# Two adaLN transformer layers, main attention: the place of the next heads' query weights (their fetch and their split) moved by one prepared block

## The chip, the cores and the metric

The kernel runs on one core of one Trainium2 chip. The metric is the time of one execution on the device in microseconds; the median of three runs is given. All times inside the program are counted from the start of the profiled span.

## The reference

One call computes two transformer layers on an input of 1024 rows by 256. Only the first half of the first layer matters here, its main attention over 16 heads:

```python
q = (q_mid @ q_b_w.T).reshape(b, s, H, D_Q).transpose(0, 2, 1, 3)
q_nope, q_pe = (q[..., :D_NOPE], q[..., D_NOPE:])
kv_lora, k_pe_flat = (kv_a[..., :KVR], kv_a[..., KVR:])
...
q_pe = apply_rope(q_pe, cos, sin)
k_pe = apply_rope(k_pe, cos, sin)
qf = jnp.concatenate([q_nope, q_pe], -1)
kf = jnp.concatenate([k_nope, k_pe], -1)
scores = jnp.einsum('bhqd,bhkd->bhqk', qf, kf) * scale
probs = jax.nn.softmax(scores.astype(jnp.float32), axis=-1).astype(dt)
ctx = jnp.einsum('bhqk,bhkd->bhqd', probs, v)
main_out = ctx.transpose(0, 2, 1, 3).reshape(b, s, H * D_V) @ o_w.T
```

Here s is 1024, H 16, D_NOPE 128, D_ROPE 64. A pattern attention before it, a gated feed-forward of eight experts behind it and the whole second layer are not touched.

## The kernel before

**Tiles and units.** The main attention goes by pairs of heads, p = 0 to 7, and within a pair by four units of 256 queries each, so units u = 0 to 31 with p = u // 4. A unit has four score tiles (two heads, two times 128 queries) of 128 by 1024. For a tile PE multiplies queries with keys in three passes (L1834 to L1836: high with high, high with low, low with high), DVE takes the maxima (`nmq`, L1843), ACT exponentiates (`P`, L1858), DVE turns the result (`PT`, L1871), and PE multiplies it with the values (L1938). ACT and DVE join the two parts (L1949, L1957), DVE weighs them (L1963), PE projects (L1972), DVE adds to `x` (L1985).

**Prepared blocks.** The scores work on latent queries and keys of 128 rows per head: 64 from the latent part and 64 rotary ones. They are prepared for one pair while the pair before is in hand, in six blocks of 128 by 512, in this order: R0, R1 (rotary keys, two halves of the columns), R2 (rotary queries, first half), Q0 (latent queries, first half), R3, Q1 (second halves). In the code this is `FIRST`, k = 0 to 5. For each block

- PE computes the product (`pe_prep`, L1569) once the split weights are there: `wkh`/`wkl` for R0 and R1, `wqh`/`wql` for R2 and R3, `lth`/`ltl` for Q0 and Q1;
- ACT copies it from its bank to a staging tile `t` (L1623), of which there are two, taken in turn;
- for a rotary block SP issues four DMAs that swap rows of 32 within the tile (L1637), behind the copy;
- POOL (`pool_product`) multiplies by the cosine (L1650), by the sine behind the swap (L1652), adds (L1655), and writes the high halves (L1669) and low halves (L1676) of two heads, `qk1h`/`qk1l` for keys and `qk0h`/`qk0l` for queries. Latent blocks have the last two steps only.

The score tiles of pair p begin with score(4p, 0). It waits (`pe_score`) for R0, R1, R2 and Q0 of the pair, high and low; the second half of the queries, score(4p + 2, 0), waits for R3 and Q1.

**The order.** `main_order` writes out one list, MAIN, and each engine walks it and takes what is its own. With `PREP_AT = (5, 8, 9, 12, 16, 17)` the product of block k of pair p stands at score tile 16(p − 1) + PREP_AT[k]: R0 in unit 4p − 3, R1 and R2 in unit 4p − 2, Q0 in unit 4p − 1, R3 and Q1 in unit 4p. In a unit the order is

```python
order.append(("score", u, 0))
output(u - 2)
prep(4 * u, "prep")
order.extend([("rec", u - 1), ("spread", u - 1), ("vturn", u - 1, 3), ("expo", u, 0)])
prep(4 * u, "pcopy")
```

and then the tiles 1 to 3 with the two halves of the value product of unit u − 1. "rec" is DVE's row of reciprocals (`rrow`) and SP's four DMAs that gather it (`shares`, L1906); "spread" is SP's two DMAs that spread it to `Rs` (L1919), behind the first. SP's queue is strictly in order: the swap of a block stands behind the shares and the spread of its unit. POOL does not follow MAIN for this part. It has its own loop over pairs and blocks (`gpsimd`), so it is only as far as its own work and waits let it.

**The weights.** `wks` and `wqs` hold 128 by 256 of rotary weights of one pair, fetched by one DMA each (`sp_weights_k`, `sp_weights_q`) behind PE's last use of the ones before. POOL splits them into `wkh`, `wkl` (L1736, L1738) and `wqh`, `wql` (L1745, L1747); the latent weights are split into `lth`, `ltl` (L1756, L1758). The semaphore `wt_ok` counts the splits in the order key, latent, query of each pair.

Of the kernel before, what the change touches and what calls it, by code (L numbers as in the profile page):

```python
# [307 lines left out]
def program(nc, a, out):  # L308
# [1217 lines left out]
    def pool_mc(e, l):  # L1526
        e.wait_ge(ht_mm, 8 + 8 * l)
        e.memset(mc[0][:].bitcast(F32), 0.0).then_inc(mc_ok, 1)
        e.memset(mc[1][:].bitcast(F32), 0.0).then_inc(mc_ok, 1)
        e.wait_ge(mc_ok, 2 * l + 2)  # L1530
        if l:
            e.memset(mc[0][:, :, 96:99].bitcast(F32), 1.0).then_inc(mc_ok, 1)
            e.memset(mc[1][:, :, 96:99].bitcast(F32), 1.0).then_inc(mc_ok, 1)
# [186 lines left out]
    def sp_weights_k(e, p):  # L1720

        if p:
            e.wait_ge(rp_mm, 4 * p - 2)
        e.dma_start(wks[:], a["wkpe"][p]).then_inc(d_wk, 16)

    def sp_weights_q(e, p):

        if p:
            e.wait_ge(rp_mm, 4 * p)
        e.dma_start(wqs[:], a["wqpe"][p]).then_inc(d_wq, 16)  # L1730
# [10 lines left out]
    def pool_weights_q(e, p):  # L1741
        e.wait_ge(d_wq, 16 * (p + 1))
        if p:
            e.wait_ge(rp_mm, 4 * p)
        e.tensor_copy(wqh[:], wqs[:]).then_inc(wt_hi, 1)  # L1745
        e.wait_ge(wt_hi, SPLIT2["q", p])
        e.tensor_tensor(wql[:], wqs[:], wqh[:].bitcast(F32), ALU.subtract).then_inc(wt_ok, 1)  # L1747
        e.wait_ge(wt_ok, SPLIT2["q", p])

    def pool_weights_l(e, p):  # L1750
        if p:
            e.wait_ge(lt_mm, 2 * p)
        else:
            e.wait_ge(fold_ok, 6)
            e.wait_ge(d_below, 32)
        e.tensor_copy(lth[:], wab[:, :, 2 * p:2 * p + 2, :].rearrange("p a h c -> p a (h c)")).then_inc(wt_hi, 1)  # L1756
        e.wait_ge(wt_hi, SPLIT2["lat", p])
        e.tensor_tensor(ltl[:, :, p, :], wab[:, :, 2 * p:2 * p + 2, :].rearrange("p a h c -> p a (h c)"), lth[:].bitcast(F32), ALU.subtract).then_inc(wt_ok, 1)  # L1758
        e.wait_ge(wt_ok, SPLIT2["lat", p])
# [116 lines left out]
    def sp_values(e):  # L1876

        e.wait_ge(sh_mm, 16)
        e.wait_ge(pv_mm[0], 128)
        for s in range(4):  # L1880
            for g in range(4):
                e.dma_start(kv4[s][32 * g:32 * g + 32, :, :], kvx[32 * s:32 * s + 32, :, :]).then_inc(d_kv, 16)
# [1146 lines left out]
    def gpsimd(e):  # L3029
        pool_mc(e, 0)  # L3030
        pool_stack2(e, slice(0, 4))
        pool_vx_ones(e, 0)
        pool_latents(e)
        e.wait_ge(qkv_ok, NT)
        e.wait_ge(fold_ok, 6)
        pool_stack2(e, slice(4, 8))
        pool_rounded(e)
        pool_weights_k(e, 0)
        pool_weights_q(e, 0)
        pool_weights_l(e, 0)  # L3040
        e.wait_ge(neg_ok, 8)
        pool_scale(e)
        for p in range(8):
            if p < 2:
                pool_keys(e, p)
            for k in range(len(FIRST)):
                pool_product(e, p, k)
                if k == 0 and p:
                    pool_weights_q(e, p)
                elif k == 3 and p < 7:  # L3050
                    pool_weights_k(e, p + 1)
                elif k == 5 and p < 7:
                    pool_weights_l(e, p + 1)
        for s in MAIN:
            if s[0] == "wup":
                pool_scale_down(e, s[1])
            elif s[0] == "wdown":
                pool_split_down(e, s[1])
            elif s == ("hT", 0):
                pool_hT1(e)  # L3060
            elif s[0] == "hidden":
                pool_up0(e, *s[1:])
        e.wait_ge(dn_mm, downs_done(5))
        pool_vx_ones(e, 1)
        pool_mc(e, 1)
        for s in CAUSAL:
            if s[0] == "omm":
                pool_op_gate(e, s[1])
            elif s[0] == "split":
                pool_split1(e, s[1])  # L3070
            elif s[0] == "turn3":
                pool_hTh3(e)
        pool_fill1(e)
        for s in FINAL:
            if s[0] == "omm":
                pool_op_gate(e, s[1])
            elif s[0] == "split":
                pool_split1(e, s[1])
            elif s[0] == "hid" and KIND[s[1]] is None:
                pool_hidden1(e, *s[1:])  # L3080

    def sync(e):
        e.dma_start(idf[:], a["idf"]).then_inc(d_c, 16)
        e.dma_start(cc[:], a["cc"]).then_inc(d_c, 16)
        for i in range(2):
            e.dma_start(x[:, 4 * i:4 * i + 4, :], x_v[:, 4 * i:4 * i + 4, :]).then_inc(d_x[i], 16)
        e.dma_start(wm0[:, :, 0:512], a["wmod0"][:, :, 0:512]).then_inc(d_moda, 16)
        e.dma_start(wsp[:, 0:2, :, :], a["wsp0"][:, 0:2, :, :]).then_inc(d_w, 16)
        e.dma_start(owT[:], a["owT"]).then_inc(d_w3[0], 16)
        e.dma_start(kvbv[:], a["kvbv"]).then_inc(d_w3[0], 16)  # L3090
        e.dma_start(wm0[:, :, 512:1536], a["wmod0"][:, :, 512:1536]).then_inc(d_modb, 16)
        e.dma_start(w0a[:], a["w0a"]).then_inc(d_w2, 16)
        e.dma_start(lnw[:, 0:192], a["q_ln"].partition_broadcast(128)).then_inc(d_w2, 16)
        e.dma_start(lnw[:, 192:256], a["kv_ln"].partition_broadcast(128)).then_inc(d_w2, 16)
        e.dma_start(gsb[:], a["gate_b"].partition_broadcast(128)).then_inc(d_w2, 16)
        e.dma_start(wsp[:, 2:4, :, :], a["wsp0"][:, 2:4, :, :]).then_inc(d_wv, 16)
        sp_scratch2(e, 0)
        sp_scratch2(e, 1)
        sp_stack2(e, 0)
        e.dma_start(qbn[:], a["qbn"]).then_inc(d_w3[1], 16)  # L3100
        e.dma_start(kvbk[:], a["kvbk"]).then_inc(d_w3[1], 16)
        for d, n in ((idb, "idb"), (maskq, "maskq"), (maskk, "maskk"), (tri, "tri")):
            e.dma_start(d[:], a[n]).then_inc(d_k, 16)
        sp_stack2(e, 1)
        e.wait_ge(gate_mm, 4)
        e.wait_ge(gate_v, 8)
        sp_weights_k(e, 0)
        sp_weights_q(e, 0)
        sp_scratch2(e, 2)
        sp_scratch2(e, 3)  # L3110
        sp_stack2(e, 2)
        e.dma_start(cosT[:], a["cosT"]).then_inc(d_cs, 16)
        e.dma_start(sinT[:], a["sinT"]).then_inc(d_cs, 16)
        sp_below(e)
        for k in range(len(FIRST)):
            sp_swap(e, 0, k)
            if k == 2:
                sp_weights_k(e, 1)
        sp_values(e)
        for s in MAIN:  # L3120
            if s[0] == "pcopy":
                sp_swap(e, s[1], s[2])
                if s[2] == 0:
                    sp_weights_q(e, s[1])
                elif s[2] == 2 and s[1] < 7:
                    sp_weights_k(e, s[1] + 1)
            elif s[0] == "rec":
                if s[1] == 28:
                    e.wait_ge(st_mm[1], 16 * 7)
                    e.dma_start(wr[:], a["wr"]).then_inc(d_f, 16)  # L3130
                    e.dma_start(tmpr[:, 0:1], a["temp"].partition_broadcast(128)).then_inc(d_f, 16)
                    for x_ in range(2):
                        sp_expert0(e, x_)
                sp_shares(e, s[1])
            elif s[0] == "spread":
                sp_spread(e, s[1])
        for x_ in range(2, 4):
            sp_expert0(e, x_)
        e.wait_ge(*MAIN_DONE)
        e.dma_start(wm1[:], a["wmod1"]).then_inc(d_moda, 16)  # L3140
        e.wait_ge(ht_mm, 16)
        e.dma_start(w1a[:], a["w1a"]).then_inc(d_w1a, 16)
        e.dma_start(bcol[:], a["bqk"]).then_inc(d_w1a, 16)
        e.dma_start(bvr[:], a["bvr"]).then_inc(d_w1a, 16)
        e.dma_start(bob[:], a["bo"].partition_broadcast(128)).then_inc(d_w1a, 16)
        for x_ in range(4, 8):
            sp_expert0(e, x_)
        sp_stacks(e)

        e.wait_ge(st_mm[0], TILEP[1][3, 1, 7, 1][0] + 1)  # L3150
        e.dma_start(cen[:], a["cen"]).then_inc(d_f, 16)
        e.dma_start(bib[:], a["ebias"].partition_broadcast(128)).then_inc(d_f, 16)
        e.dma_start(b1c[:], a["b1c"]).then_inc(d_f, 16)
        e.dma_start(selt[:], a["sel"]).then_inc(d_f, 16)
        for f in range(NF):
            sp_expert1(e, f)
        sp_finish(e)
# [138 lines left out]
```

## Time and profile before

| what | us |
|---|---|
| runs: median (lowest to highest) | 1307.02 (1306.5 to 1322.74) |
| profiled execution, on the device | 1305.7 |
| its span | 1303.9 |
| PE busy in the span | 1188.6 |
| DVE busy | 882.3 |
| ACT busy | 652.4 |
| POOL busy | 531.8 |
| main attention, from the first score of unit 2 to that of unit 28 | 291.29 to 702.32 |

PE is TensorE, DVE VectorE, ACT ScalarE, POOL GpSimd, SP SyncE, which issues all DMAs. The mean granted clock of PE over the span is 0.971 of full speed. In the views of waits and in the timelines a bracket such as `[5.24 <-POOL wql L1747]` says how long the engine stood idle before the row and what released it. S(u) in the text is the start of the first score matmul (L1834) of unit u.

### The profile page before, as it was taken

Reading aid. Unit: us, or ns where it says so; the run is one execution under the profiler, and the core shown is the slowest. Engines: PE = TensorE matmul, PEld = TensorE weight load, DVE = VectorE, ACT = ScalarE, POOL = GpSimd, SP = SyncE. Lnnn points to the kernel's source line nnn. Section 1 sums busy time; section 2 is a strip of 40 time slices with the busy share of each in tenths; the row PEclk is TensorE's granted clock in tenths of the full one; section 3 lists DMA queues with packets and bytes.
Section 4 is the critical chain, followed back from the end, with each engine's and each line's share of the span. In section 5 each row is a group of like instructions: output and inputs, shape, how many; then the busy total and the mean of one; then the engine's idle time right before and its main releaser. Section 6 shows DMA issues by size and latency. Waiting matters only on the chain.

```text
span 1303.9 us, 34626 instructions
## 1 busy us (share of the span) xinstructions
PE 1188.6 (91%) x14436; PEld 830.6 (64%) x14436; DVE 882.3 (68%) x1354; ACT 652.4 (50%) x1242; POOL 531.8 (41%) x531
## 2 busy tenths in 40 slices
PE   8999999997989889898988869999998998999997
PEld 5544334465767667676766657788853444678997
DVE  4689988366768676776776775744667764665555
ACT  3469978853434343343433334333245767445553
POOL 4257264228485766667565422445200000421221
PEclk8989999999989999998998988999999999999999
DMA  7880000011111111101010113010231510101110
GB/s 274 207 178 2 2 17 21 1 47 34 31 31 32 31 31 31 39 25 45 24 41 20 60 35 113 25 42 33 72 86 50 108 38 1 33 17 33 50 41 33
DMA packets 41699, 66.25 MB, mean 51 GB/s; under 512 B 8476, under 2 KB 27676, under 8 KB 40604
## 3 DMA queue, kind: packets, MB, share of 16 engines
q1 hardware_dynamic: 41544, 64.04, 18.1%
q8 instruction: 115, 1.88, 0.6%
q14 instruction: 40, 0.33, 0.1%
HBM read 45.60 MB, written 8.45 MB: 41 GB/s over the span
## 4 chain that ended last, share of the span: by engine, by line
PE 63%; DVE 13%; POOL 9%; issue 5%; ACT 4%; SPq 3%; DMA 3%; ACTq 0%; POOLq 0%; DVEq 0%
PE bank L1478 8%; PE bank L1938 6%; PE bank L2148 6%; PE bank L2149 6%; PE bank L2150 6%; PE bank L1435 4%; PE bank L1569 3%; PE bank L1298 3%; PE bank L1834 3%; PE bank L1835 2%; PE bank L1836 2%; PE bank L1415 2%; DMA t<-t 2%; DVE mpc L1377 2%; POOL qk0l L1676 2%
## 5 line engine op out<-in xcount | busy, mean ns | idle before, releaser
L1858 ACT ACTIVATE P<-bank,nmq 128x1024 f32<-128x1024 f32 x128 | 142.7, 1115 | 142.4 <-DVE nmq L1843 140.8
L1843 DVE TENSOR_REDUCE nmq<-bank 128x1 f32<-128x1024 f32 x128 | 153.2, 1197 | 84.6 <-PE bank L1836 84.4
L1456 ACT ACTIVATE Pb<-bank 128x512 f32<-128x512 f32 (+3 forms) x355 | 180.6, 574 | 31.8 <-PE bank L1435 11.0
L1306 DVE TENSOR_REDUCE mp<-bank 128x2 f32<-128x1024 f32 x128 | 153.5, 1222 | 29.9 <-PE bank L1298 29.1
L1871 DVE STREAM_TRANSPOSE PT<-P 128x1024 f32<-128x1024 f32 x124 | 151.6, 1223 | 0.9 <-ACT P L1858 0.9
L1938 PE MATMUL bank<-PT,kv 32*64 32x128 f32 x7936 | 136.5, 276 | 7.3 <-issue 6.9
L1938 PEld LDWEIGHTS bank<-PT,kv 32*64 32x64 f32 x7936 | 118.9, 131 | 33.5 <-issue 33.5
L1834 PE MATMUL bank<-qk1h,qk0h 128*128 128x512 f32 x256 | 113.6, 444 | 15.0 <-ACT P L1858 7.9
L1377 DVE TENSOR_REDUCE mpc<-bank 128x2 f32<-128x1024 f32 (+2 forms) x96 | 88.3, 953 | 43.0 <-PE bank L1365 22.0
L1478 PE MATMUL bank<-Pb,vx 128*17 128x256 f32 (+3 forms) x1222 | 106.3, 408 | 0.7 <-ACT OTa L1492 0.5
L1836 PE MATMUL bank<-qk1h,qk0l 128*128 128x512 f32 x256 | 103.6, 405 | 0.7 <-issue 0.7
L1835 PE MATMUL bank<-qk1l,qk0h 128*128 128x512 f32 x256 | 103.7, 405 | 0.0
L1652 POOL TENSOR_TENSOR t<-t,sinT 128x512 f32<-128x512 f32 x32 | 41.1, 1284 | 95.4 <-DMA t<-t 95.4
L2123 POOL TENSOR_TENSOR cTt<-cTt,gab 128x256 f32<-128x256 f32 x8 | 6.1, 757 | 180.3 <-DVE cTt L2118 180.0
L2349 POOL TENSOR_TENSOR hl<-hf,hh 128x512 fp32r<-128x512 f32 x32 | 41.2, 1288 | 90.8 <-ACT hh L2336 90.8
L1834 PEld LDWEIGHTS bank<-qk1h,qk0h 128*128 128x128 f32 x256 | 50.0, 195 | 38.0 <-issue 15.9
L1435 PE MATMUL bank<-qstr,kstr 64*128 64x512 f32 x256 | 71.5, 499 | 0.6 <-ACT Pb L1456 0.6
L1650 POOL TENSOR_TENSOR Rt<-t,cosT 128x512 f32<-128x512 f32 x32 | 41.1, 1284 | 75.2 <-ACT t L1623 72.9
L2563 POOL TENSOR_TENSOR v1l<-wr,v1h 128x512 fp32r<-128x512 f32 x25 | 32.1, 1286 | 95.1 <-ACT v1h L2558 95.1
L1949 ACT ACTIVATE other<-bank 64x256 f32<-64x256 f32 x64 | 24.2, 378 | 87.9 <-PE bank L1938 87.1
L1435 PEld LDWEIGHTS bank<-qstr,kstr 64*128 64x128 f32 x256 | 28.3, 184 | 58.0 <-ACT Pb L1456 36.6
L1623 ACT ACTIVATE t<-bank 128x512 f32<-128x512 f32 x48 | 28.5, 594 | 66.5 <-PE bank L1569 66.5
(354 smaller groups left out, 2926.9 us busy)
## 6 DMA issues: line engine op xcount, KB each, us to landing
t<-t SPq DMA_DIRECT2D x128, 64.0 KB, 2.0
wr<-wf SPq DMA_DIRECT2D x25, 256.0 KB, 2.7
wraw<-wf SPq DMA_DIRECT2D x8, 768.0 KB, 4.5
scratch<-stgr SPq DMA_DIRECT2D x4, 1024.0 KB, 4.0
Rs<-shares SPq DMA_DIRECT2D x64, 64.0 KB
scratch<-stg SPq DMA_DIRECT2D x8, 384.0 KB, 2.6
qst<-scratch SPq DMA_DIRECT2D x9, 256.0 KB, 8.1
owT<-owT SPq DMA_DIRECT2D x1, 2048.0 KB, 11.6
```

The lines of the kernel that those rows point to most:

```text
L1306: e.tensor_reduce(mp[:, w % 3, :, j, kh], wide[slot][:], AX, ALU.max).then_inc(ring_ok, 1)
L1377: e.tensor_reduce(mpc[:, w // 2 % 3, a0:a0 + 2, j, kh], wide[slot][:, :, 0:c], AX, ALU.max).then_inc(ring_ok, 1)
L1435: e.matmul(bank[b][:], kst2[r, hp, kt * 128:kt * 128 + 128], qst2[r, hp, cols(half)], start=True, stop=True).then_inc(st_mm[0], 1)
L1456: e.activation(PBR[l][i % len(PBR[l])][:, 0:c], bank[b][:, 0:c], ACT.Exp, scale=0.25).then_inc(exp_ok[0], 1)
L1478: last = e.matmul(bank[6][32 * a:32 * a + 17, to:to + c], vx[:, t, h * 17:h * 17 + 17], PBR[l][i % len(PBR[l])][:, q0:q0 + c], start=(t == ...
L1834: e.matmul(o, qh[:, qs], kh[:, ks], start=True, stop=False)
L1835: e.matmul(o, qh[:, qs], kl[:, ks], start=False, stop=False)
L1836: last = e.matmul(o, ql[:, qs], kh[:, ks], start=False, stop=True)
L1843: e.tensor_reduce(nmq[:, n % 8:n % 8 + 1], scores(u, i), AX, ALU.max, negate=True).then_inc(mp_ok, 1)
L1858: e.activation(probabilities(u, i)[:], scores(u, i), ACT.Exp, bias=nmq[:, n % 8:n % 8 + 1], accum_out=sums[:, u % 2, i:i + 1]).then_inc(ex ...
L1871: e.transpose(PT[u % 2][:, :, c:c + 32], source).then_inc(pt_ok, 1)
L1938: last = e.matmul(rest[64 * c:64 * c + 64, g, 64 - 64 * c:192 - 64 * c], kv4[b % 4][rows, b // 4, :], transposed(u, b)[rows, :], start=(b ...
```

## The change

The fetch and the split of the query weights of pair p + 1 are moved. On POOL the split stood behind the first product (R0) of the pair that uses it; now it stands behind the latent split that follows the last product (Q1) of the pair before. On SP the fetch stood behind the swap of R0; now it stands at Q1's place in the list, one unit earlier, behind the swap of R3. That of pair 1 stands ahead of the copies of the values.

```diff
                 pool_product(e, p, k)
-                if k == 0 and p:
-                    pool_weights_q(e, p)
-                elif k == 3 and p < 7:
+                if k == 3 and p < 7:
                     pool_weights_k(e, p + 1)
                 elif k == 5 and p < 7:
                     pool_weights_l(e, p + 1)
+                    pool_weights_q(e, p + 1)
...
             if k == 2:
                 sp_weights_k(e, 1)
+        sp_weights_q(e, 1)
         sp_values(e)
         for s in MAIN:
             if s[0] == "pcopy":
                 sp_swap(e, s[1], s[2])
-                if s[2] == 0:
-                    sp_weights_q(e, s[1])
+                if s[2] == 5 and s[1] < 7:
+                    sp_weights_q(e, s[1] + 1)
```

POOL's instructions between the last block of pair 1 and block R1 of pair 2, before (numbers behind a name tell copies of a tile apart):

```order
L1756 CAST lth<-wab 128x256
L1758 TENSOR_TENSOR ltl<-wab,lth 128x2x128
L1650 TENSOR_TENSOR Rt<-t_152,cosT 128x512
L1652 TENSOR_TENSOR t_152<-t_152,sinT 128x512
L1655 TENSOR_TENSOR Rt<-Rt,t_152 128x512
L1669 CAST qk1h_138<-Rt 64x512
L1669 CAST qk1h_139<-Rt 64x512
L1676 TENSOR_TENSOR qk1l_146<-Rt,qk1h_138 64x512
L1676 TENSOR_TENSOR qk1l_147<-Rt,qk1h_139 64x512
L1745 CAST wqh<-wqs 128x256
L1747 TENSOR_TENSOR wql<-wqs,wqh 128x256
L1650 TENSOR_TENSOR Rt<-t_153,cosT 128x512
```

and the same place of POOL in the changed kernel:

```order
L1756 CAST lth<-wab 128x256
L1758 TENSOR_TENSOR ltl<-wab,lth 128x2x128
L1745 CAST wqh<-wqs 128x256
L1747 TENSOR_TENSOR wql<-wqs,wqh 128x256
L1650 TENSOR_TENSOR Rt<-t_152,cosT 128x512
L1652 TENSOR_TENSOR t_152<-t_152,sinT 128x512
L1655 TENSOR_TENSOR Rt<-Rt,t_152 128x512
L1669 CAST qk1h_138<-Rt 64x512
L1669 CAST qk1h_139<-Rt 64x512
L1676 TENSOR_TENSOR qk1l_146<-Rt,qk1h_138 64x512
L1676 TENSOR_TENSOR qk1l_147<-Rt,qk1h_139 64x512
L1650 TENSOR_TENSOR Rt<-t_153,cosT 128x512
```

The two instructions of the split have passed the seven of R0; the cosine product of R1 has the same number of instructions ahead of it as before.

SP's queue from the swap of R3 of pair 1 (unit 4) to the swaps of R1 and R2 of pair 2 (unit 6), before:

```order
L1906 DMA shares<-rrow 4x32 x4
L1919 DMA Rs<-shares 64x2x128 x2
L1637 DMA t_152<-t_152 32x512 x4
L1906 DMA shares<-rrow 4x32 x4
L1919 DMA Rs<-shares 64x2x128 x2
L1637 DMA t_152<-t_152 32x512 x4
L1730 DMA wqs<-wqpe 128x256
L1906 DMA shares<-rrow 4x32 x4
L1919 DMA Rs<-shares 64x2x128 x2
L1637 DMA t_153<-t_153 32x512 x4
L1637 DMA t_152<-t_152 32x512 x4
```

and in the changed kernel:

```order
L1906 DMA shares<-rrow 4x32 x4
L1919 DMA Rs<-shares 64x2x128 x2
L1637 DMA t_152<-t_152 32x512 x4
L1730 DMA wqs<-wqpe 128x256
L1906 DMA shares<-rrow 4x32 x4
L1919 DMA Rs<-shares 64x2x128 x2
L1637 DMA t_152<-t_152 32x512 x4
L1906 DMA shares<-rrow 4x32 x4
L1919 DMA Rs<-shares 64x2x128 x2
L1637 DMA t_153<-t_153 32x512 x4
L1637 DMA t_152<-t_152 32x512 x4
```

The fetch has passed the swap of R0 and the shares and the spread ahead of it. PE, DVE and ACT have the same instructions in the same order.

## Rows read from the trace of the kernel before

**Rows 1.** The page's busy time, share of the span and instructions of each engine.

```profile
PE 1188.6 (91%) x14436; PEld 830.6 (64%) x14436; DVE 882.3 (68%) x1354; ACT 652.4 (50%) x1242; POOL 531.8 (41%) x531
```

**Rows 2.** Waits of PE, 270 to 880 us: waited for, us in total, times, longest.

```profile
PE bank L1569 <- POOL wql L1747: 32.6, 7, 5.2
...
PE bank L1834 <- POOL qk0l L1676: 6.3, 3, 5.1
```

**Rows 3.** Timeline of PE: start, us, engine, line, operation [idle before].

```profile
328.45 0.50 PE L1834 MATMUL bank<-qk1h,qk0h 128*128 128x512 f32 x1
...
355.54 0.47 PE L1834 MATMUL bank<-qk1h,qk0h 128*128 128x512 f32 x1 [0.48 <-POOL qk0l L1676]
...
366.05 0.76 PE L1569 MATMUL bank<-qah,wqh 128*128 128x512 f32 x1 [5.24 <-POOL wql L1747]
...
390.43 0.50 PE L1834 MATMUL bank<-qk1h,qk0h 128*128 128x512 f32 x1
...
404.13 0.50 PE L1834 MATMUL bank<-qk1h,qk0h 128*128 128x512 f32 x1
...
417.37 0.50 PE L1834 MATMUL bank<-qk1h,qk0h 128*128 128x512 f32 x1
...
450.77 0.47 PE L1834 MATMUL bank<-qk1h,qk0h 128*128 128x512 f32 x1
...
667.18 0.50 PE L1834 MATMUL bank<-qk1h,qk0h 128*128 128x512 f32 x1
...
702.32 0.76 PE L1834 MATMUL bank<-qk1h,qk0h 128*128 128x512 f32 x1 [5.15 <-POOL qk0l L1676]
...
719.90 0.50 PE L1834 MATMUL bank<-qk1h,qk0h 128*128 128x512 f32 x1
```

**Rows 4.** Timeline of POOL, 344 to 390 us: R3 of pair 1 to Q0 of pair 2.

```profile
344.34 1.29 POOL L1652 TENSOR_TENSOR t<-t,sinT 128x512 f32<-128x512 f32 x1 [8.59 <-DMA t<-t]
...
352.55 2.62 POOL L1676 TENSOR_TENSOR qk0l<-t,qk0h 64x512 fp32r<-64x512 f32 x2
...
355.72 0.74 POOL L1758 TENSOR_TENSOR ltl<-wab,lth 128x256 fp32r<-128x256 f32 x1
356.53 1.28 POOL L1650 TENSOR_TENSOR Rt<-t,cosT 128x512 f32<-128x512 f32 x1
...
364.60 0.40 POOL L1745 CAST wqh<-wqs 128x256 fp32r<-128x256 f32 x1
...
365.87 1.28 POOL L1650 TENSOR_TENSOR Rt<-t,cosT 128x512 f32<-128x512 f32 x1
369.43 1.28 POOL L1652 TENSOR_TENSOR t<-t,sinT 128x512 f32<-128x512 f32 x1 [2.28 <-DMA t<-t]
...
385.81 2.64 POOL L1676 TENSOR_TENSOR qk0l<-t,qk0h 64x512 fp32r<-64x512 f32 x2
```

**Rows 5.** Timeline of SP's queue, 351 to 373 us.

```profile
360.80 2.14 SPq L1906 DMA_DIRECT2D shares<-rrow  x4
363.98 1.35 SPq L1919 DMA_DIRECT2D Rs<-shares  x2
365.43 6.99 SPq L1637 DMA_DIRECT2D t<-t  x8
```

**Rows 6.** Timeline of POOL: low half of Q0 of pairs 1, 3 and 7.

```profile
321.71 2.60 POOL L1676 TENSOR_TENSOR qk0l<-t,qk0h 64x512 fp32r<-64x512 f32 x2
...
447.77 2.64 POOL L1676 TENSOR_TENSOR qk0l<-t,qk0h 64x512 fp32r<-64x512 f32 x2
...
699.27 2.60 POOL L1676 TENSOR_TENSOR qk0l<-t,qk0h 64x512 fp32r<-64x512 f32 x2
```

**Rows 7.** Stretch, us; busy PE, PEld, DVE, ACT, POOL; PEclk (granted), DMA share, GB/s.

```profile
302.00:305.50 3.50, 3.50 (x9) 2.73 (x10) 0.00 (x0) 1.16 (x2) 1.25 (x2) 0.53 0.38 97
...
675.80:680.00 4.20, 4.19 (x114) 3.44 (x122) 2.17 (x3) 1.80 (x4) 1.12 (x1) 1.00 0.18 51
702.30:708.40 6.10, 6.08 (x14) 4.80 (x15) 2.60 (x6) 1.21 (x2) 0.00 (x0) 0.50 0.00 0
```

## The prediction

> **What bounds the kernel now.** I read the page's line of engines first: PE is busy for 1188.6 of 1303.9 us [rows 1], so only something that keeps PE from waiting, or from a low clock, can move the time. The waits of PE in the stretch of the main attention come next: the largest is that of the preparing products (L1569) for `wql`, POOL's split of the query weights, 32.6 us in 7 waits, one per head pair; score products waited for `qk0l`, POOL's last write of a prepared block, 6.3 us in 3 [rows 2]. Then PE's timeline, by the first score matmul of a unit. S(u) is the start of unit u. For pair 2 (its blocks are prepared in units 5 to 9, its scores begin at S(8)) S(4) is 328.45, S(6) 355.54, the waiting block is computed at 366.05 after 5.24 us of wait, and S(8) is 390.43 [rows 3]. So two ordinary units take 27 us (390.43 to 417.37 likewise), and the two that hold the wait take 34.9. POOL's timeline shows why `wql` is late, and something more: POOL multiplies by the sine of R3 of the pair before at 344.34, after 8.59 us of wait for the swapped rows, ends Q1 at 355.17, splits the latent weights until 356.46, does R0, splits the query weights from 364.60 on, begins R1 at 365.87, waits for its swapped rows until 369.43, and then works without a pause through R1, R2 and Q0, whose low half ends at 385.81 + 2.64 = 388.45 [rows 4]. Score(8, 0) needs exactly that Q0. The same release costs 0.37 us from POOL's end to PE's start (355.17 to 355.54), so S(8) could not be before 388.82, and it was 390.43. The rows on which the argument hangs are therefore not those of the wait that goes, but those of the next one.
>
> **The change, part by part.**
>
> 1. The two instructions of the split keep their number, form and cost: `wqh` and `wql` take from 364.60 to 365.87, 1.3 us, between R0 and R1 of a pair [rows 4]. They now stand behind the latent split of the pair before, thus from 356.53 to about 357.8 in pair 2. PE comes to the block at 366.05 − 5.24 = 360.81, so it finds `wql` 3 us old: the 32.6 us of waits go, all seven.
>
> 2. The DMA of the weights (one issue) goes ahead by one unit: behind the swap of R3, when SP would otherwise stand idle, instead of behind the swap of R0. Its wait (rp_mm at 4 products of the pair) is met before R3's swap can begin. In pair 2 it is issued right behind the swap of R3, which has landed at 344.34; a swap takes 4 us from issue to the product that waits for it (365.43 to 369.43 for R1 [rows 4, 5]), so the weights are there by about 348, and POOL wants them at 356.5. I cost it at nothing; if it were late, POOL would stand before R0, but 8 us of cover would have to be gone first. What is queued behind it on SP is the next shares and spread.
>
> 3. Does POOL reach the end of Q0 sooner? R0 starts 1.3 us later, and the split that stood behind it is gone, so R1's cosine product still starts at 365.87. Its sine product waits for the swap until 369.43 whatever POOL does: SP issues the swaps of R1 and R2 in one run from 365.43, right behind the spread at 363.98, which follows the shares at 360.80 [rows 5]. These belong to the reciprocal row of unit 5, computed by DVE behind S(6), and move only if S(6) moves. So Q0 ends at 388.45 as before, and S(8) is 388.82: a gain of 1.61 us, not of 5.24. In this accounting the second half of a pair, S(4p−2) to S(4p), becomes 33.3 us (355.54 to 388.82). That of pair 3 is 450.41 + 0.37 − 417.37 = 33.4, which is what it already was (S(12) = 450.77) [rows 3, 6].
>
> 4. The slack between Q0's end plus 0.37 and S(4p), for the pairs 1 to 7: 3.77 (Q0's low half ends at 321.71 + 2.60, S(4) is 328.45), 1.61, 0, 1.48, 0.47, 1.72, 0 (699.27 + 2.60 against 702.32, where 5.15 us of wait stand already) [rows 3, 6]. Sum 9.05 us. The two other waits for `qk0l`, 6.3 − 5.15 = 1.1 us (one is the 0.48 before 355.54), are those of S(4p+2) for Q1 [rows 2, 3]; they go too if PE comes later there. Together 10.1 us gained.
>
> 5. What is added: PE now arrives at score(4p, 0) about 27 us behind S(4p−2) and waits there for Q0. Pair 7 shows the size: with a wait of only 2.75 us for `wql` it arrived at 702.32 − 5.15 = 697.17, that is 30.0 us behind S(26) = 667.18, or 27.2 without that wait [rows 3]. So the new wait is 33.3 − 27.2 = 6 us per pair. After waits of 4.8 to 5.2 us the granted clock is 0.50 (1.2 GHz); after the one of 2.75 us it stays at 1.00 [rows 7]. Seven low stretches begin with the work behind a wait and last 3.5, 4.5, 4.0, 3.5, 6.0, 5.5 and 6.1 us (the first and the last are shown). Their mean is 4.7; matmuls of 128x512 follow each other at twice the distance there, so half, 2.4 us, is lost each time. Before, six of these losses lay in the second half of a pair, where POOL is late anyway and hides them in part. Now they lie in the first half, S(4p) to S(4p+2), which is on the closed chain: S(4p+2) → reciprocal row → shares, spread, swap of R1 → R1, R2, Q0 on POOL → S(4p+4). I call the loss E. It occurs behind S(4), S(8), ... S(24), six times; behind S(28) it is there already. Bounds: 0, if the loss is absorbed by units 4p and 4p+1; 3.9, which is what unit 28 took after its wait (719.90 − 702.32 = 17.58) above unit 8 (404.13 − 390.43 = 13.70) [rows 3]. I take the half of the mean low stretch, 2.4, since PE is the engine without a pause in unit 8. 6 × 2.4 = 14.4 us added.
>
> Sum: −10.1 + 14.4 = +4.3 us. The profiled execution took 1305.7 us (span 1303.9), so 1310.0; the median of the runs is 1.3 us above it, so I say 1311. The bounds of E give −10.1 and +13.3, or 1297 and 1320. About 2% (26 us) is what a measurement of this kernel tells from no change.
>
> A rule for the clock: the Trainium skill, TensorE: Matmul & The Clock Gate, section HAM oscillation, says that idle waits between bursts throttle PE again each time, at a cost of half the throttled time, and that one should shape the loop so that the waits don't occur. Read alone, it would pay this change the wait and the half of all seven stretches. The trace agrees with the halving; the rule says nothing of a wait that comes back one unit and a half later.
>
> **The rivals.**
>
> A. The wait simply goes. Then 32.6 us are saved and half of the six low stretches behind waits for `wql`, 27 / 2 = 13.5: 1305.7 − 46.1 = 1259.6, about 1261 as a median. For it: PE's busy share, and 32.6 us is the largest wait that PE has in the stretch. Against it: S(8) would have to be 390.43 − 5.24 − 2.4 = 382.8, with Q0 ending at 388.45 [rows 4]. It needs the swap of R1 some 6 us sooner. The clock rule named above favours it. 7%.
>
> B. The wait moves, but the low clock costs nothing: DVE and ACT catch up during the new wait, the weighing and the transpose that PE otherwise waits for are then ready, and two units absorb the rest. That leaves −10.1: 1295.6, or 1297 as a median. For it: no row of before shows this wait followed by units without other work. Against: unit 28 came out 3.9 us longer behind it, and a low stretch behind a wait is in the rows each time the wait is near 5 us. 11%.
>
> C. Slower: the new wait at score(4p, 0) leaves PE, DVE and ACT in lockstep for two units rather than one, each as long as unit 28 behind the one wait of this sort, 17.58 us against 13.70 [rows 3]. That is 7.8 us per pair: 46.8 − 10.1 = +36.7, or 1344 as a median. It decides (over 2%) from 6.0 us per pair on, (26 + 10.1) / 6. Against: a low stretch of 3.5 to 6.1 us lies in one unit only, and losing half of it can't make 7.8. 5%.
>
> D. The weights come no earlier: the DMA sits behind SP's other waits, or POOL waits for it before R0. Then `wql` is still waited for, and the time stays near 1307. Against: 8 us of cover (step 2). 2%.
>
> **How the numbers follow.** The forecast (the wait moves, E between 1 and 3.9) has 75%, B 11%, A 7%, C 5%, D 2%. Time 1311; range 1295 to 1322, which takes in B, D and both bounds of E. Faster by over 2% is A alone, 0.07; slower by over 2% is C alone, 0.05; the rest, 0.88, is within.
>
> **What would show it.** In the changed kernel's waits of PE no row for `wql`, and instead a row of score products (L1834) for `qk0l` with 7 waits and some 6 us each, near 44 us in all. S(6) to S(8) and its like 33 to 34 us; S(8) to S(10) 28 to 31 instead of 27. A granted clock of 0.50 in the first microseconds of units 4, 8, ... 28, none in units 6, 10, .... R1's sine product still released by the swap, 14 us behind S(4p+2). POOL's wait for the copy of R3 about as long as before. I am wrong if the swap of R1 lands sooner than 13 us behind the start of its unit, if PE's waits for `qk0l` sum to under 25 us, or if PE's clock stays up behind them.

## The result, and the profile after

Over 20 executions each, in the same rounds, the changed kernel took 1317.64 us in the median (1312.1 to 1325.18), the kernel before 1312.29 (1304.23 to 1322.74). The ratio is 1.0044, with a 95% interval of 1.0025 to 1.0063: 5.8 us slower, less than the 2% that the forecast called the limit of what matters, but clear of noise. The median of before is 5 us above the one of the three runs that the forecast started from. The profiled execution of before (1305.7 us) was one of the quickest; that of the changed kernel (1319.2 us, span 1317.4) lies near its median. So differences between the two profiles (13.5 us of span) are larger than the true one, and I use them for where the time lies, not for how much it is in all.

The busy times are those of before [rows 1] to within 5 us; PE did the same work in a longer span:

```profile
PE 1188.7 (90%) x14433; PEld 835.2 (63%) x14436; DVE 886.9 (67%) x1354; ACT 652.9 (50%) x1242; POOL 531.7 (40%) x531
```

PE's waits in the changed kernel, 270 to 880 us (us in total, times, longest):

```profile
PE bank L1834 <- POOL qk0l L1676: 47.7, 7, 9.1
PE bank L1972 <- DVE OTm L1963: 13.7, 23, 3.8
```

The row for `wql` of [rows 2], 32.6 us, is gone. The row for `qk0l`, which had 6.3 us in 3 waits, has 47.7 in 7: one per pair. Removed: 32.6. Added: 41.4.

PE's timeline shows where, as first score matmuls of units 4, 6, 8, 9, 10, 12, 26, 28 and 29, against [rows 3]:

```profile
326.41 0.76 PE L1834 MATMUL bank<-qk1h,qk0h 128*128 128x512 f32 x1 [4.12 <-POOL qk0l L1676]
...
355.19 0.50 PE L1834 MATMUL bank<-qk1h,qk0h 128*128 128x512 f32 x1
...
389.20 0.77 PE L1834 MATMUL bank<-qk1h,qk0h 128*128 128x512 f32 x1 [6.41 <-POOL qk0l L1676]
...
404.58 0.50 PE L1834 MATMUL bank<-qk1h,qk0h 128*128 128x512 f32 x1
...
417.89 0.47 PE L1834 MATMUL bank<-qk1h,qk0h 128*128 128x512 f32 x1
...
453.97 0.77 PE L1834 MATMUL bank<-qk1h,qk0h 128*128 128x512 f32 x1 [9.06 <-POOL qk0l L1676]
...
675.88 0.50 PE L1834 MATMUL bank<-qk1h,qk0h 128*128 128x512 f32 x1
...
711.92 0.77 PE L1834 MATMUL bank<-qk1h,qk0h 128*128 128x512 f32 x1 [8.98 <-POOL qk0l L1676]
...
728.06 0.50 PE L1834 MATMUL bank<-qk1h,qk0h 128*128 128x512 f32 x1
```

S(4) to S(6) is 28.8 us, S(8) to S(10) 28.7, where 27.1 and 26.9 stood; S(10) to S(12) is 36.1 and S(26) to S(28) 36.0, where 33.4 and 35.1 stood. Unit 28, which had this wait already, takes 16.1 us instead of 17.6. Each head pair begins with a wait of 4 to 9 us, and its first matmul takes 0.76 or 0.77 us where it took 0.50: PE's clock has fallen in the wait. The granted clock (the column of 0.50 and 1.00) in the first microseconds of units 4, 8 and 12 and, for comparison, of unit 26, where no wait stands:

```profile
326.40:330.40 4.00, 3.99 (x10) 3.15 (x11) 1.06 (x1) 0.00 (x0) 0.84 (x2) 0.50 0.00 0
389.20:393.60 4.40, 4.40 (x11) 3.46 (x11) 1.23 (x1) 0.20 (x1) 0.83 (x2) 0.50 0.00 0
453.90:458.70 4.80, 4.73 (x11) 3.83 (x12) 1.31 (x2) 0.54 (x1) 0.89 (x2) 0.50 0.02 3
675.80:680.00 4.20, 3.92 (x27) 2.92 (x17) 3.09 (x5) 1.96 (x4) 3.78 (x4) 1.00 0.02 4
```

POOL's timeline for pair 2, the counterpart of [rows 4]:

```profile
353.37 0.73 POOL L1758 TENSOR_TENSOR ltl<-wab,lth 128x256 fp32r<-128x256 f32 x1
354.17 0.40 POOL L1745 CAST wqh<-wqs 128x256 fp32r<-128x256 f32 x1
354.64 0.73 POOL L1747 TENSOR_TENSOR wql<-wqs,wqh 128x256 fp32r<-128x256 f32 x1
355.45 1.28 POOL L1650 TENSOR_TENSOR Rt<-t,cosT 128x512 f32<-128x512 f32 x1
...
364.35 1.27 POOL L1650 TENSOR_TENSOR Rt<-t,cosT 128x512 f32<-128x512 f32 x1 [0.17 <-POOL qk1l L1676]
369.89 1.28 POOL L1652 TENSOR_TENSOR t<-t,sinT 128x512 f32<-128x512 f32 x1 [4.28 <-DMA t<-t]
...
386.25 2.59 POOL L1676 TENSOR_TENSOR qk0l<-t,qk0h 64x512 fp32r<-64x512 f32 x2
```

The split is done before R0, as intended. POOL gets to R1 1.5 us sooner than before and waits 4.28 instead of 2.28 us for R1's swapped rows, so Q0's low half ends at 388.84; score(8, 0) starts 0.36 us later. SP's queue, against [rows 5]:

```profile
340.50 0.58 SPq L1730 DMA_DIRECT2D wqs<-wqpe  x1
...
360.48 2.14 SPq L1906 DMA_DIRECT2D shares<-rrow  x4
363.67 1.35 SPq L1919 DMA_DIRECT2D Rs<-shares  x2
365.12 6.26 SPq L1637 DMA_DIRECT2D t<-t  x8
```

Here the new fact is small and turned out to matter: the swap of R1 was issued at 365.12 and its user started at 369.89, 4.77 us later. Before it was 365.43 and 369.43, 4.00 us.

By halves of a pair, read from the same timelines (S(u) as before; "landing" is the time from the first issue of R1's swap to POOL's sine product):

| | S(4p) to S(4p+2), mean of 6 | S(4p−2) to S(4p), mean of 7 | landing, pairs 1 to 7 |
|---|---|---|---|
| before | 27.7 | 35.0 | 4.01 4.00 4.00 4.00 4.24 4.00 4.75 |
| changed | 29.0 | 35.3 | 5.04 4.77 5.16 4.93 4.93 5.08 6.41 |

Six first halves are 8.0 us longer, seven second halves 1.8. That is the 9.6 us by which S(28) moved (702.32 to 711.92), since S(2) stands 0.15 us earlier (291.14 instead of 291.29).

### The profile page after: what moved, and what is told of

Its sections match the earlier page's. It is cut to its first block, busy times and chain, and to the rows that moved or that the text cites. A ratio compares the mean times of both kernels' runs of the same rounds, so it can differ in the third digit from the quotient of the medians.

```text
span 1317.4 us, 34623 instructions
## 1 busy us (share of the span) xinstructions
PE 1188.7 (90%) x14433; PEld 835.2 (63%) x14436; DVE 886.9 (67%) x1354; ACT 652.9 (50%) x1242; POOL 531.7 (40%) x531
## 4 chain that ended last, share of the span: by engine, by line
PE 61%; DVE 13%; POOL 12%; issue 4%; ACT 4%; SPq 3%; DMA 3%; POOLq 0%; ACTq 0%; DVEq 0%
PE bank L1478 7%; PE bank L2148 6%; PE bank L2149 6%; PE bank L2150 6%; PE bank L1938 5%; PE bank L1435 4%; POOL qk0l L1676 3%; PE bank L1569 3%; PE bank L1834 3%; PE bank L1298 3%; PE bank L1836 2%; PE bank L1835 2%; DMA t<-t 2%; PE bank L1415 2%; DVE mpc L1377 2%
## 5 line engine op out<-in xcount | busy, mean ns | idle before, releaser
L1456 ACT ACTIVATE Pb<-bank 128x512 f32<-128x512 f32 (+3 forms) x355 | 180.7, 574 | 31.6 <-PE bank L1435 10.7
L1834 PE MATMUL bank<-qk1h,qk0h 128*128 128x512 f32 x256 | 114.3, 447 | 59.6 <-POOL qk0l L1676 47.7
L1938 PE MATMUL bank<-PT,kv 32*64 32x128 f32 x7936 | 135.7, 275 | 8.6 <-issue 7.7
L1938 PEld LDWEIGHTS bank<-PT,kv 32*64 32x64 f32 x7936 | 118.3, 130 | 34.0 <-issue 33.8
L1415 PE MATMUL bank<-qst,kst 107*128 107x512 bf16 (+3 forms) x192 | 53.8, 330 | 7.9 <-ACT qst L1402 3.5
```

Source lines behind the costliest of these rows:

```text
L1456: e.activation(PBR[l][i % len(PBR[l])][:, 0:c], bank[b][:, 0:c], ACT.Exp, scale=0.25).then_inc(exp_ok[0], 1)
L1834: e.matmul(o, qh[:, qs], kh[:, ks], start=True, stop=False)
L1938: last = e.matmul(rest[64 * c:64 * c + 64, g, 64 - 64 * c:192 - 64 * c], kv4[b % 4][rows, b // 4, :], transposed(u, b)[rows, :], start=(b ...
```

## The experiments

The changed kernel's theory: a chain sets the period, from S(4p−2) over the reciprocal row, shares, spread and swap of R1 to POOL's R1, R2 and Q0 and to S(4p), and on to S(4p+2), where the low clock behind the new wait is added. The rivals: POOL or SP as such, or the clock alone.

**1. One part alone: the fetch.** POOL as in the kernel before, SP as in the changed one.

```diff
+        sp_weights_q(e, 1)
         sp_values(e)
...
-                if s[2] == 0:
-                    sp_weights_q(e, s[1])
+                if s[2] == 5 and s[1] < 7:
+                    sp_weights_q(e, s[1] + 1)
```

> One part of the change alone: SP fetches the next query weights one unit earlier, POOL splits them where it did before. Theory: the split's place is all that matters; wql is waited for 7 times, 4.7 us each, as before, ratio 0.998 to 1.002. Rival (the fetch at its new place disturbs SP or the DMAs): ratio above 1.002, with S(4p-2) to S(4p) longer.

Ratio 0.9995 (0.9966 to 1.0024), 1310.23 us. The waits are those of before; R1's landing is 3.98 to 4.01 us in five pairs of seven.

```profile
PE bank L1569 <- POOL wql L1747: 32.2, 7, 5.3
```

With the split at its old place the fetch neither gives nor costs anything within the interval's 0.3% either way, as said in step 2.

**2. The other part alone: the split.** POOL as in the changed kernel, SP as in the one before.

```diff
-                if k == 0 and p:
-                    pool_weights_q(e, p)
...
+                    pool_weights_q(e, p + 1)
```

> The other part of the change alone: POOL splits the next query weights behind the latent split, SP fetches them where it did before, behind R0's swap. Theory: POOL stands about 2 us before R0 until the weights land, R0 ends some 3 us later than before, still no later than the swap of R1 lands, so Q0 is not moved; the wait for wql goes and that for Q0 comes as in the changed kernel: ratio 1.002 to 1.008. Rival (the place of the fetch matters): ratio above 1.01 or below 1.0.

Ratio 1.0086 (1.005 to 1.0121), 1320.59 us: just above the 1.002 to 1.008 that I expected, and the interval reaches into the rival's range (above 1.01). It also overlaps that of the whole change (1.0025 to 1.0063), so that the times alone don't show this kernel to be the slower one. The wait for `wql` is gone, that for `qk0l` is 45.3 us in 7. In the profile, which caught the slowest of its five executions, the excess up to S(28) lies in pair 1, where S(2) to S(4) is 40.5 us instead of 35.3. There POOL waits for the fetch behind R0's first swap and starts R0 at 299.28 (284.89 in the changed kernel), and PE stands 5.64 us before a value product for an ACT copy that this holds up. In pairs 2 to 7 the halves are in the mean those of the changed kernel. So the split's place makes the effect, and what the earlier fetch adds is to spare pair 1 this delay, as one trace shows.

**3. PE kept at work in part of the new wait.** The changed kernel with dummy products ahead of score(4p, 0)'s wait; they are read by nobody.

```diff
+        if i == 0 and u % 4 == 0 and u:
+            e.wait_ge(*free)
+            for _ in range(14 if u == 4 else 22):
+                e.matmul(wide[slot][:, 0, :], qah[:, 0:128], qah[:, 0:512], start=True, stop=True)
         if i == 0 and u % 2 == 0:
             e.wait_ge(rp_hi, 4 * p + 3 + half)
```

> The changed kernel, with PE kept at work in part of the new wait: ahead of the wait of score(4p, 0) for Q0 it multiplies 22 times (14 in unit 4) a tile of constant latent queries with itself into the bank that this score overwrites. The dummy products are left without a reader, the output is the same. Theory (the low clock behind the wait lies on the closed chain from S(4p) to S(4p+2)): the granted clock stays at 1.00 in units 4, 8, ... 28, S(4p) to S(4p+2) goes from 28.7 to 29.4 us back to 27 to 28, and the kernel is about 1.5 us faster per pair than the changed one: 6 x 1.5 + 2 behind S(28) = 11 us, a ratio of 0.995 to 0.998 against the kernel before. Rival (the first half grew for another reason, or POOL alone sets the period): a ratio of 1.003 to 1.006 as for the changed kernel.

Ratio 0.9997 (0.9974 to 1.0021), 1308.5 us. That is 0.0047 below the changed kernel, 6 us where I had said 11; between the two expectations, nearer to the theory. The six first halves last 27.6 us in the mean, down from 29.0; the second halves stay at 35.2. The clock was not kept up everywhere, since some wait was left behind the dummies (16.6 us in 6 waits). In pair 2 it fell in 3.94 us of wait (the first row has the last 5 of the 22 dummies):

```profile
383.70 1.29 PE L1824 MATMUL bank<-qah 128*128 128x512 f32 x5
388.93 0.76 PE L1838 MATMUL bank<-qk1h,qk0h 128*128 128x512 f32 x1 [3.94 <-POOL qk0l L1676]
389.50 0.63 PE L1839 MATMUL bank<-qk1l,qk0h 128*128 128x512 f32 x1
```

The mean of 27.6, as long as before, is therefore a mixture. In pairs 3, 4 and 6 the granted clock is 1.00 over the whole first half, and it lasts 26.4, 26.3 and 25.9 us; in pairs 1, 2 and 5 the clock fell (waits of 3.0 to 4.1 us), and it lasts 30.6, 27.9 and 28.5. The first halves of pairs 3, 4 and 6 took 29.1 us in the mean in the changed kernel and 28.2 before. So the low clock is on the chain, and it costs more than the first halves had grown by: without it, a first half behind a wait (or behind the dummies in its place) is shorter than before the change.

**4. The same dummies in the kernel before**, in its wait for `wql`.

```diff
         e.wait_ge(pc_ok, len(FIRST) * p + k - 1)
+        if k == 2:
+            for _ in range(8 if p == 7 else 18):
+                e.matmul(bank[b][:], qah[:, 0:128], qah[:, 0:512], start=True, stop=True)
         pe_part(e, p, FIRST[k], bank[b][:], (0, 1))
```

> The kernel before, with the same 18 dummy products (8 in pair 7) in its wait for the query weights, ahead of the product of R2. Theory: the clock stays up in units 6, 10, ..., which brings PE some 2 us sooner to S(4p); there only the slack of 0 to 3.8 us against Q0's end can be taken, so about 1.3 us per pair, 7 to 9 us in all, ratio 0.993 to 0.996. A wait for qk0l of 0 to 2 us appears at S(4p). Rival (the clock behind this wait costs nothing since POOL is late anyway): ratio 0.999 to 1.001.

Ratio 0.9952 (0.9932 to 0.9972), 1304.21 us, as expected. The wait at S(4p) appears as soon as PE comes 2 us sooner:

```profile
PE bank L1569 <- POOL wql L1750: 6.5, 6, 2.8
PE bank L1837 <- POOL qk0l L1679: 5.3, 5, 2.0
```

In this kernel Q0 was only 0 to 3.8 us from being the bound, and no more than that could be had.

**5. Is the longer landing of R1's swap due to R2's?** R2's copy is ready early in the changed kernel, so its four DMAs follow R1's at once. The changed kernel, with SP waiting for the one before it issues the other.

```diff
         t = staging(p, k)
+        if k == 2 and p:
+            e.wait_ge(*SWAPS[p, 1])
         for q in range(4):
```

> The changed kernel, with one wait more on SP: the swap of R2 is issued only when the swap of R1 has landed. Theory (R1's swap lands 4.8 to 5.1 us behind its issue in the changed kernel and 4.0 in the one before, because R2's copy is ready early and its four DMAs follow at once and share the way): the swap of R1 is back at 4.0, S(4p-2) to S(4p) shrinks by 0.9 us per pair, 6 to 7 us in all, ratio 0.998 to 1.001 against the kernel before. R2's swap lands some 4 us later, still ahead of its use 8 us behind R1's. Rival (the delay lies in the issues on SP or in DVE's reciprocal row, not in R2's DMAs): landing stays near 5 us, ratio 1.003 to 1.006.

Ratio 1.0046 (1.0026 to 1.0065), 1315.76 us; landing 4.91, 5.11, 5.47, 4.62, 4.82, 4.90 and 4.47 us, a mean of 4.9 where the changed kernel has 5.2 and the one before 4.1. My explanation fell: R2's DMAs are not the cause.

**6. Is it PE's own progress?** With the wait for `wql` gone, PE is in its value products (L1938) while R1's rows are swapped. The first of them starts 8.2 to 8.8 us behind S(4p−2) in the changed kernel, and 14.8 to 15.7 before (pairs 1 to 6). So I put a hold where the removed wait stood: the dummies of experiment 4 in the changed kernel, 4.2 us of useless work per pair.

```diff
+        if k == 2:
+            for _ in range(8 if p == 7 else 18):
+                e.matmul(bank[b][:], qah[:, 0:128], qah[:, 0:512], start=True, stop=True)
         pe_part(e, p, FIRST[k], bank[b][:], (0, 1))
```

> The changed kernel, with PE held back where the removed wait stood: 18 dummy products (8 in pair 7; constant latent queries with themselves, into the bank of the product of R2, which overwrites them) ahead of R2's product, 4.2 us of PE work. Theory (in the changed kernel PE runs its value products, 128 small instructions each, while R1's rows are swapped; then the spread and the swap are issued and land slower, 4.8 to 5.2 us instead of 4.0; with PE in the dummies instead, they don't): R1's swap lands 4.0 us behind its issue, S(4p-2) to S(4p) is 33.3 instead of 35.3 us, the wait for Q0 falls to about 2 us, the clock stays up and S(4p) to S(4p+2) is 27 to 28. Then a kernel with 4.2 us of useless work more per pair is faster than the changed one by 6 x 3 = 18 us or somewhat less: ratio 0.990 to 0.997 against the kernel before. Rival (the longer landing comes from something else, the earlier copies of R2 or the later R0 on POOL): landing stays near 5 us; then only the clock is gained, ratio 0.999 to 1.002.

Ratio 0.995 (0.9926 to 0.9974), 1303.28 us: useless work makes the changed kernel 0.9% faster, and faster than the one before. The wait for `qk0l` fell from 47.7 to 12.2 us in 3. Landing is 4.01, 3.98, 4.86, 3.99, 5.44, 4.70 and 5.06 us: 4.0 in three pairs, not in the others. The view of DMAs gives a hint at what differs. During the swap of R1 of pair 3, before and then changed:

```profile
q1 hardware_dynamic: 480, 0.39, 37.5%
```

```profile
q1 hardware_dynamic: 369, 0.39, 30.2%
q8 instruction: 1, 0.02, 1.7%
```

The changed kernel has a transfer on the instruction queue in it; 1.7% of 16 engines' time over the 5.16 us is 1.4 us of one of them. All seven pairs of seven kernels (before, changed, experiments 1 and 3 to 6) give 49 swaps. Of the 19 without a transfer of queue 8 all landed in 3.98 to 4.24 us; of the 30 with one, 27 took 4.47 to 6.41 us and 3 took 4.0. In these three the transfer began 3.7 to 3.9 us behind the first issue, when the swap was all but through. The queue's name doesn't say whose instructions it carries. Its number of transfers points to PE: 115 of 16 KB in either kernel, one for about 250 of PE's 28,872 matmuls and weight loads, where the other engines have some 3,100 instructions together. PE's value products are 128 matmuls in 2 us, the densest stretch of them, and when PE gets there sooner, such a transfer falls into the swap. That is a coincidence seen 46 times in 49, not an isolated cause: I had no edit that moves the transfer alone. In the same pairs the spread was often issued more slowly too, 2.13 us for its two DMAs in pair 3 instead of 1.33.

**7. The chain cut.** The changed kernel with R1's swap ahead of the shares and the spread of its unit on SP.

```diff
+    SP_MAIN = list(MAIN)
+    for p_ in range(1, 8):
+        n_ = SP_MAIN.index(("pcopy", p_, 1))
+        m_ = max(i_ for i_ in range(n_) if SP_MAIN[i_][0] == "rec")
+        SP_MAIN.insert(m_, SP_MAIN.pop(n_))
...
-        for s in MAIN:
+        for s in SP_MAIN:
             if s[0] == "pcopy":
```

> The changed kernel, with R1's swap ahead of the shares and the spread of its unit on SP. Theory (the chain S(4p-2) -> reciprocal row -> shares -> spread -> swap of R1 -> POOL's R1, R2, Q0 -> S(4p) sets the period): R1's sine product starts about 11 us behind S(4p-2), as POOL gets there, instead of 15.7; Q0 ends near +30.5; S(4p-2) to S(4p) is 30 to 31 us instead of 35.3, the wait for Q0 is 3 to 4 us instead of 6.8, and in part of the pairs the clock stays up. 4.5 x 7 = 32 us, less some for the spread that comes 3 us later: 1280 to 1292 us, ratio 0.975 to 0.987. Rival (POOL's own work is the bound, or the spread comes too late for the weighing and PE waits there instead): ratio 0.995 to 1.005.

Ratio 0.9761 (0.9729 to 0.9793), 1276.72 us, as expected. SP and POOL in pair 2: the swap goes first, and R1's sine product follows its cosine product without a wait.

```profile
350.64 2.41 SPq L1637 DMA_DIRECT2D t<-t  x4
353.14 2.14 SPq L1906 DMA_DIRECT2D shares<-rrow  x4
356.34 1.35 SPq L1919 DMA_DIRECT2D Rs<-shares  x2
357.79 3.02 SPq L1637 DMA_DIRECT2D t<-t  x4
```

```profile
353.82 1.27 POOL L1650 TENSOR_TENSOR Rt<-t,cosT 128x512 f32<-128x512 f32 x1 [0.17 <-POOL qk1l L1676]
355.04 1.29 POOL L1652 TENSOR_TENSOR t<-t,sinT 128x512 f32<-128x512 f32 x1
```

The second halves are 30.2 us in the mean instead of 35.3, and the first 27.9 instead of 29.0. The waits at S(4p) are 2.4 us and less, and the clock's loss is smaller but not gone: in pairs 2 to 5, behind waits of 1.1 to 2.4 us, the granted clock fell for 3.4 us each, as in pair 2 here, and in pairs 1 and 6 it stayed at 1.00.

```profile
375.60:378.90 3.30, 3.30 (x9) 2.53 (x9) 1.99 (x3) 1.21 (x2) 0.00 (x0) 0.50 0.00 0
```

```profile
PE bank L1834 <- POOL qk0l L1676: 8.9, 5, 2.4
```

**8. The same edit in the kernel before.**

> The kernel before, with R1's swap ahead of the shares and the spread of its unit on SP. Theory: Q0 ends 2.4 us sooner, but S(4p) was set by PE in all pairs but the third and the seventh, since the wait for wql stays; 0 to 4 us gained, ratio 0.995 to 1.001. With the run of the changed kernel with the same edit it shows that the removed wait and the swap each give nothing alone and much together. Rival (the swap alone is the bound): ratio below 0.99.

Ratio 0.9992 (0.9968 to 1.0016), 1309.45 us, as expected.

```profile
PE bank L1569 <- POOL wql L1747: 32.7, 7, 5.2
...
PE bank L1834 <- POOL qk0l L1676: 0.4, 1, 0.4
```

With 7 the four corners are there: neither edit 1, the change 1.0044, the swap 0.9992, both 0.9761. Two bounds lay behind each other in the same half of a pair; taking either away gave nothing.

**9. Wait kept, clock kept up, swap first.** The kernel before with the edits of 7 and 4.

> The kernel before with R1's swap ahead of the shares and the spread, and the 18 dummy products (8 in pair 7) in its wait for wql. The wait is still there, only the clock stays up behind it. Theory: PE reaches S(4p) about 2 us sooner, at S(4p-2) + 32.5 to 33, where Q0, done at +32, is ready: 7 x 2 = 14 us less than the kernel before, ratio 0.987 to 0.992. That would be half of what removing the wait gives with the same swap (0.976), the other half being the wait itself. Rival (the swap edit and the change don't act on one chain, and the clock explains it all): ratio near 0.976.

Ratio 0.99 (0.987 to 0.9929), 1297.57 us, as expected. Of the 2.4% that the change and the swap give together, about 1% comes with the clock behind the wait alone; the rest, by difference, is the wait itself.

**10. Is R3's swap on the chain as well?** As 7, with R3's swap also ahead (`itertools.product(range(1, 8), (1, 4))` in the loop).

> The changed kernel with the swaps of both R1 and R3 ahead of the shares and the spread of their units. With R1's alone the kernel took 1276.7 us and PE still waited about 2 us for Q0 at S(4p), where S(4p-2) to S(4p) is 30.2 us. Theory: R3's swap is not on the chain (PE sets S(4p) to S(4p+2), and R1's sine product waits for its own swap, whose copy is made at S(4p-2) + 5.4 us): POOL gets earlier through R3, Q1 and R0 and waits longer for R1. Same time within 3 us, ratio 0.974 to 0.979. Rival (POOL's arrival at R1 was the bound, so that all POOL work from R3 on counts): 2 to 3 us less per pair, ratio 0.960 to 0.970.

Ratio 0.9727 (0.9695 to 0.976), 1276.2 us. That is just under the lower end of what the theory said, and its interval overlaps that of 7; the rival's 2 to 3 us per pair are not there. A small gain stays open. The kernel of 7 and this one are the fastest measured.

## Why the prediction was right, point by point

- **The wait goes and comes back (steps 1, 3 and 5).** Right. The 32.6 us for `wql` went, 47.7 us for `qk0l` came in 7 waits of 4.1 to 9.1 us; I had said 6 us each, near 44.
- **The fetch costs nothing (step 2).** Right; experiment 1 measured it alone (0.9995, 0.9966 to 1.0024).
- **"Its sine product waits for the swap until 369.43 whatever POOL does" (step 3).** The bound is the right one, which experiments 7 and 8 show, but its time is not independent of PE. R1's sine product started 14.7 to 16.8 us behind S(4p−2), not 14. Second halves are 35.3 us in the mean instead of the 33.7 that step 4 comes to, which cost the whole gain of 9.05 us and 1.8 us more. This is the term that I missed, 1.5 us per pair, two thirds of it the landing. The likely cause is a transfer of instructions in the same moment, probably PE's (experiment 6), seen but not isolated; R2's DMAs are excluded (experiment 5).
- **E, the low clock on the chain (step 5).** The mechanism is right: where experiment 3 kept the clock up, the loss went. The first halves grew by 8.0 us, or 9.1 with the 1.1 us of waits for Q1 that step 4 took off, so E is 1.5 us per pair instead of 2.4. The low stretch itself was sized well: behind S(4), S(8), ... S(24) it lasts 3.3 to 6.1 us, 5.1 in the mean, of which half is 2.5 (4.7 and 2.4 in step 5), and experiment 3 puts the loss at 2.8, 29.0 against the 26.2 of the three halves with the clock up. What step 5 left out is that a first half behind a wait needs less: 26.2 us against 27.5 before (27.7 less the waits for Q1). The sums over the six first halves, before and then changed, show part of it:

```profile
sum 166.00, PE 158.06 PEld 123.82 DVE 133.08 ACT 78.03 POOL 76.90; mean PE 26.34 PEld 20.64 DVE 22.18 ACT 13.01 POOL 12.82
```

```profile
sum 173.96, PE 170.15 PEld 134.66 DVE 125.42 ACT 65.14 POOL 87.29; mean PE 28.36 PEld 22.44 DVE 20.90 ACT 10.86 POOL 14.55
```

  PE is busy for 12.1 us more, and its idle time falls from 7.9 to 3.8 us. Of these 4.1 us, 1.1 are the waits for Q1 and 1.7 waits for the weighing, which DVE now does during the wait at S(4p): that of unit 6 starts 5.0 us ahead of S(8), at 384.18, where before it started 1.5 us behind it, at 391.88. DVE's busy time in these halves falls by 7.7 us.
- **The sum.** −10.1 + 14.4 = +4.3 by my steps; the profiles give +1.8 for the second halves and +8.0 for the first. The missed term adds 10.9 us and the smaller E takes off 5.3, and behind S(28) another 3.9 us of the 13.5 lie that I attribute to nothing; the 20 runs say +5.8 us. The forecast of a small loss inside 2% holds, partly by luck, since two errors of size had opposite signs. The absolute forecast of 1311 is below 1317.6 mostly because three runs had shown before at 1307 and twenty show it at 1312.
- **The rivals.** A (1260 us) fell with the result. It would have needed R1's swap 6 us sooner; experiment 7 issued it 4.8 us sooner (5.9 instead of 10.7 us behind S(4p−2)), and the kernel took 1276.7 us. B (the clock costs nothing) fell with experiment 3. C (two slow units) fell: unit 9, behind unit 8, is ordinary, 404.58 to 417.89 or 13.3 us. D fell with the waits. The Trainium skill's rule in TensorE: Matmul & The Clock Gate, HAM oscillation, holds at the new place as at the old: each of the waits of 4.1 to 9.1 us is followed by a stretch of 2.8 to 6.1 us at a granted clock of 0.50 (1.2 GHz). It says what a wait costs, not which wait comes next.

## What to carry to other kernels

Before removing a wait, look up when the next thing that the waiting engine needs is ready; here the slack of Q0 (0 to 3.8 us per pair, 9 us in all) was the most that the edit could give, and for each pair it stood in two rows. Where an in-order queue carries a small urgent transfer behind bookkeeping that nobody awaits soon, put the urgent one first: that edit was worth nothing alone and 2.4% with the other. A wait of an engine can be moved to a worse place. Keeping the clock up behind the old wait shortened S(2) to S(28) by 7.8 us, 1.1 per pair (experiment 4); behind the new one it gave 2.9 us in each of the three pairs in which it worked (experiment 3). Over the whole kernel both experiments gave the same 0.5%; in the changed kernel the clock still fell in the four other pairs.

## What the runs showed that I had not expected

Four DMAs of one swap landed in 4.0 to 4.2 us when no transfer of the instruction queue ran beside them, and in 4.5 to 6.4 us in 27 of the 30 cases where one did. And 4.2 us of useless matmuls per pair made the changed kernel 0.9% faster. In the profiles (experiment 6) the six first halves are 7.3 us shorter for it, with the clock up in half of them, and the seven second halves 5.9 us, with R1's swap landing in 4.6 us in the mean instead of 5.2.
